# Expert stage of a routed feed-forward layer: 64 tiles of 96 slots against 48 tiles of 128 slots

## What is computed

```python
x = x + tanh(g_xattn) * attention(layernorm(x), ctx)      # channels 128, softmax over 256 keys
t = layernorm(x)                                          # T = 2048 tokens of 256
scores = softmax(t @ gate.T)                              # E = 64 experts, best 3 of 8 groups, top K = 6
pos  = running count of tokens at each expert
slot = expert * C + min(pos, C - 1)                       # C = 96 slots each
buf[slot] = t[token]                                      # the last slot keeps its newest token
out[e] = (silu(buf[e] @ Wg[e].T) * (buf[e] @ Wu[e].T)) @ Wd[e].T     # 256 -> 176 -> 256
y = sum over 6 of out[slot] * weight
x = x + tanh(g_ffn) * (y + shared(t))
```

## Time and profile before

| what | value |
|---|---|
| time, median of 3 runs | 437.4 us (434.9 to 438.97) |
| the profiled execution's own time | 439.52 us |
| its span, first to last instruction | 437.8 us |
| mean granted TensorE clock | 0.946 |
| busy: PE, DVE, POOL, ACT | 342.1, 215.8, 176.3, 155.8 us |
| moved by DMA | 70.50 MB, mean 161 GB/s |

### The profile page before, as it was taken

The page is one execution under the profiler, slowest core; times in us unless marked ns, Lnnn a source line. Parts: engine busy times, 40 slices in busy tenths (PEclk is TensorE's granted clock), DMA queues, the critical chain, the costliest instruction groups (busy, mean ns, idle before and its releaser), DMA issues.

```text
span 437.8 us, 8616 instructions
## 1 busy us (share of the span) xinstructions
PE 342.1 (78%) x2589; PEld 286.3 (65%) x2589; DVE 215.8 (49%) x879; ACT 155.8 (36%) x464; POOL 176.3 (40%) x173
## 2 busy tenths in 40 slices
PE   2779598998999796998987888777968897878600
PEld 1667486876887674886866676666856775767400
DVE  5656568789588888344764111211111211157390
ACT  2566355675466311111423223322323423223000
POOL 3000011010100111022577777776777777776231
PEclk9999979999899999899999899998999999989855
DMA  8798948447100111012598999898899444444797
GB/s 296 285 337 226 266 111 263 125 131 224 58 25 6 49 31 32 25 41 81 142 261 221 250 259 259 215 231 240 216 253 255 76 77 72 73 71 57 178 298 125
DMA packets 36265, 70.50 MB, mean 161 GB/s; under 512 B 6221, under 2 KB 23401, under 8 KB 36231
## 3 DMA queue, kind: packets, MB, share of 16 engines
q1 hardware_dynamic: 21851, 50.56, 37.0%
q0 software_dynamic: 12352, 16.26, 21.2%
q10 hardware_dynamic: 2028, 3.25, 2.3%
HBM read 52.26 MB, written 17.78 MB: 160 GB/s over the span
## 4 chain that ended last, share of the span: by engine, by line
PE 22%; issue 16%; DMA 8%; DVE 7%; POOL 7%; another core or an unknown queue 3%; ACT 2%; SPq 1%; DVEq 0%; ACTq 0%; POOLq 0%
PE bank L347 20%; DMA ctx_sb<-xn_rows,gidx 3%; PE bank L582 2%; DMA w_ring<-third_rows 2%; POOL result L1548 2%; POOL even_rows L1548 2%; DMA qk_sb<-xn_rows,gidx 2%; SPq L321 1%; DMA v_sb<-xn_rows,gidx 1%; POOL third_rows L1548 1%; POOL ctx_sb L1540 1%; DVE hi_hot L1188 1%; DMA even_rows<-x_all,sidx 1%; ACT pt_sb L898 1%
## 5 line engine op out<-in xcount | busy, mean ns | idle before, releaser
L347 PE MATMUL bank<-p_sb,w_ring 128*88 128x96 f32 x1024 | 97.6, 249 | 0.6 <-issue 0.6
L347 PEld LDWEIGHTS bank<-p_sb,w_ring 128*88 128x88 f32 x1024 | 92.0, 160 | 0.9 <-issue 0.8
L1407 DVE TENSOR_TENSOR pt_sb<-pt_sb,bank 88x192 f32<-88x192 f32 x64 | 22.4, 350 | 135.1 <-ACT pt_sb L898 76.4
L1529 POOL TENSOR_SCALAR zeros<-zeros,token 128x256 f16<-128x256 f16 x16 | 14.7, 928 | 155.4 <-DVE zeros L1197 155.4
L347 PE MATMUL bank<-d_ring,pt_sb 88*96 88x256 f32 x256 | 68.7, 392 | 9.5 <-DVE pt_sb L1407 9.5
L898 ACT ACTIVATE pt_sb<-bank 88x192 f32<-88x192 f32 x64 | 20.9, 327 | 94.2 <-PE bank L347 49.7
L347 PEld LDWEIGHTS bank<-d_ring,pt_sb 88*96 88x96 f32 x256 | 37.7, 167 | 19.2 <-DVE pt_sb L1407 11.7
L1548 POOL DMA_INDIRECT even_rows<-x_all,sidx x22 | 31.7, 1439 | 13.3 <-issue 4.9
L893 ACT ACTIVATE p_sb<-bank 128x192 f32<-128x192 f32 x64 | 21.1, 329 | 42.6 <-PE bank L582 22.9
L1548 POOL DMA_INDIRECT third_rows<-x_all,sidx x21 | 30.1, 1435 | 11.1 <-issue 4.0
L1548 POOL DMA_INDIRECT result<-x_all,sidx x21 | 30.2, 1436 | 10.5 <-issue 4.3
(11 more groups left out here) (164 smaller groups left out, 593.6 us busy)
## 6 DMA issues: line engine op xcount, KB each, us to landing
w_ring<-wgu_in SPq DMA_DIRECT2D x32, 704.0 KB
d_ring<-wd_in SPq DMA_DIRECT2D x32, 352.0 KB
even_rows<-zeros SPq DMA_DIRECT2D x1, 2048.0 KB, 7.3
third_rows<-zeros SPq DMA_DIRECT2D x1, 2048.0 KB, 13.4
xn_rows<-xn SPq DMA_DIRECT2D x8, 256.0 KB, 5.0
result<-x_all SPq DMA_DIRECT2D x8, 256.0 KB, 2.2
w_ring<-even_rows SPq DMA_DIRECT2D x4, 512.0 KB, 7.0
w_ring<-third_rows SPq DMA_DIRECT2D x4, 512.0 KB, 7.9
```

Of the source, the lines that this page charges most:

```text
L347: return pe.matmul(o, lhsT, rhs, start=start, stop=stop, skip_group_check=True)
L1407: dve.tensor_tensor(act_tt[:, b % 2, :], silu_sb[:, b % 2, :], eg_ps[b % 2][:, 2 * C:4 * C], ALU.mult)\
L1529: last = pool.tensor_scalar(lo_hot[:, i, :], lo_hot[:, i, :], token1[:, at:at + 1], None, ALU.mult)
```

## The change

The 64 x 96 slots are one row of 6,144 and are cut into 48 tiles of 128; four experts fill three tiles exactly. `gidx` and `sidx` are 128 partitions by 48 tiles. Gathers and adds go by tiles, 7 tiles ahead into 9 buffers, with 4 output buffers. The scatter target is one DRAM tensor `acc_rows` with four regions of 2,176 rows; expert e adds to region e mod 4, so a tile touches two regions, and tiles that touch a common region and could hold a common token wait for each other. All four regions (8.9 MB) are filled with zeros. `down` has its weights stationary and yields the result turned; DVE copies it (`take_ot`), and PE turns it back by tile (`turn_out`). `y` stays in `x_all`: nothing is stored to `result` before the end, where the four regions are read back (2 MB each), DVE adds three to `x_all` and a matmul with the identity adds the fourth to the overflow part in PSUM, and SP stores the result plainly. Tokens lie in DRAM so that a partition's 16 rows are adjacent.

```diff
-SAVED = 4
-AHEAD = 6
-ROWS = 8
-OUTS = 8
+TILES = E * C // P
+TARGETS = 4
+TR = T + P
+AHEAD = 7
+ROWS = ROW_BLKS * EB_TILES
+OUTS = 4
+FILL = TARGETS * TR * L // P // 16
...
-            for d in (even_dram, third_dram):
-                sp.dma_start(d[0:T, :].rearrange("(p a) f -> p (a f)", p=P)
-                             .rearrange("p (a f) -> p a f", a=8), zero8).then_inc(s["fills_in"], 16)
+            for k in range(TARGETS):
+                sp.dma_start(acc_dram.rearrange("(p a) f -> p (a f)", p=P)[:, k * TARGETS * FILL:(k + 1) * TARGETS * FILL]
+                             .rearrange("p (a f) -> p a f", a=TARGETS), zero4).then_inc(s["fills_in"], 16)
...
-                    last = mm(o_ps[b % 2], act_tt[:, b % 2, m * C:(m + 1) * C],
-                              d_ring[:, bass.ds(at + m * L, L)], start=m == 0, stop=m == 1)
+                for h in range(H2):
+                    for m in range(2):
+                        last = mm(ot_ps[e % 2][:, h * C:(h + 1) * C],
+                                  d_ring[:, at + m * L + h * P:at + m * L + (h + 1) * P],
+                                  act_tt[:, e % 2, m * C:(m + 1) * C], start=m == 0, stop=m == 1)
...
+            def turn_out(t):
+                pe.wait_ge(s["ot_out"], last_expert(t) + 1)
+                wait(pe, s["o_ready"], t - 1)
+                for h in range(H2):
+                    last = pe.transpose(o_ps[t % 2][:, h * P:(h + 1) * P],
+                                        turned[t // EB_TILES % 2][:, h, P * (t % EB_TILES):P * (t % EB_TILES + 1)],
+                                        ident[:, :])
...
-            def add_up(e):
-                wait(pool, s["o_ready"], e + 1)
-
-                wait(pool, s[f"acc_in{e % 3}"], 16 * landed(e, e % 3))
+            def add_up(t):
+                pool.wait_ge(s["o_ready"], t + 1)
+
+                i = t % EB_TILES
+                if i < EB_TILES - 1 and t > 1:
+                    pool.wait_ge(s[f"acc_in{(t - 2) % OUTS}"], 16 * ((t - 2) // OUTS + 1))
+                if i == 0 and t > 2:
+                    pool.wait_ge(s[f"acc_in{(t - 3) % OUTS}"], 16 * ((t - 3) // OUTS + 1))
...
+            for r in range(PAIRS):
+                pe.wait_ge(s[f"back2_{r * QUARTERS // PAIRS}"], 16)
+                mm(sum_ps[r][:, :], ident[:, :], back[2][:, 2 * r:2 * r + 2, :].rearrange("p n f -> p (n f)"),
+                   start=False).then_inc(s["ov_done"], 1)
...
-                pool.dma_start(out[P * n * q:P * n * (q + 1), :].rearrange("(n p) f -> p n f", p=P),
-                               even_sb[:, n * q:n * (q + 1), :], accum_op=ALU.add).then_inc(s["result_added"], 16)
+                sp.dma_start(out_to[:, n * q:n * (q + 1), :], x_all[:, n * q:n * (q + 1), :]).then_inc(s["result_out"], 16)
```

More of the change, by code:

```diff
@@ L235, in build @@
[L235 to L242, removed]
+            rows_in0 rows_in1 rows_in2 rows_in3 rows_in4 rows_in5 rows_in6 rows_in7 rows_in8
@@ new lines, in wait_added, with read_back @@
+        def wait_added(eng, t):
+            for k in range(OUTS):
+                wait(eng, s[f"acc_in{k}"], 16 * len(range(k, t + 1, OUTS)))
+        def read_back(eng, k, t):
+            wait_added(eng, t)
+            n = N // QUARTERS
+            for q in range(QUARTERS):
+                eng.dma_start(back[k][:, n * q:n * (q + 1), :],
+                              acc_dram[k * TR:k * TR + T, :].rearrange("(p n) f -> p n f", n=N)[:, n * q:n * (q + 1), :])\
+                    .then_inc(s[f"back{k}_{q}"], 16)
@@ L695, in _ @@
-            for t in range(N):
-                pe.wait_ge(s["w_parts_ready"], t + 1)
-                if t // 2 == 6:
-                    pe.wait_ge(s["o_ready"], E)
-                for k, part in enumerate((high_mid, high_mid, high_low)):
-                    if k == 0 and t in early:
-                        continue
-                    last = mm(bank[t // 2][:, t % 2 * L:(t % 2 + 1) * L], part[:, t * P:(t + 1) * P],
-                              last_parts[:, k, :], start=k == 0, stop=k == 2)
-                last.then_inc(s["ov_done"], 1)
+            turn_rows(1)
@@ new lines, in _ @@
+            for e in range(1, E):
+                if e < E - 1 and last_tile(e + 1) > last_tile(e):
+                    turn_rows(last_tile(e + 1))
+                up(e)
+                down(e - 1)
+                t = last_tile(e - 2) if e > 1 else 0
+                if last_expert(t) == e - 2:
+                    turn_out(t)
+                elif t > 0 and last_expert(t - 1) == e - 2:
+                    turn_out(t - 1)
+            down(E - 1)
+            turn_out(TILES - 2)
+            turn_out(TILES - 1)
@@ new lines, in _ @@
+            take_rows(0)
+            act.wait_ge(s["ht_done"], N)
+            silu(0)
+            take_rows(1)
+            act.wait_ge(s["qk_done"], N)
+            act.wait_ge(s["h_done"], N)
+            for e in range(1, E):
+                if e < E - 1 and last_tile(e + 1) > last_tile(e):
+                    take_rows(last_tile(e + 1))
+                silu(e)
+                t = last_tile(e - 2) if e > 1 else 0
+                if last_expert(t) == e - 2:
+                    take_out(t)
+                elif t > 0 and last_expert(t - 1) == e - 2:
+                    take_out(t - 1)
```

524 lines of the change are left out of this document (282 added, 242 removed).

## The result

| what | before | changed |
|---|---|---|
| time, median (range), same chip | 438.19 us (434.9 to 439.05), 4 runs | 423.38 us (419.24 to 425.65), 4 runs |
| ratio | | 0.9672, 95% interval 0.961 to 0.9734 |
| profiled execution, span | 439.52, 437.8 us | 425.65, 423.9 us |
| second `up` of the stage to the last add | 198.2 us | 177.6 us |
| last add to the end | 31.6 us | 33.7 us |

A forecast was written before the change was run, and what follows sets the result against it. POOL's descriptor making was taken to bound the expert stage. From 439.5 us, stage - 31, opening + 12, middle + 1 and ending + 0.5 gave 422, stated as 421 because that execution ran above the median; range 407 to 443.

The forecast's parts named there:

- POOL bounds the kernel before; fewer, larger indirect transfers free it: Expert stage: POOL's descriptor making sets 2.98 us a pair; 128-row pairs would take 3.3, or 2.48 per expert.
- rival B: Expert stage: descriptors cost in proportion to rows, 3.76 us a pair, so no change at 439 us; chance 0.17.
- PE at 2.55 us is the new floor: Expert stage: PE's `up`, `down` and transposes sum to 2.55 us an expert, 160.7 us for 63.
- 160.7 + 5.5: Expert stage: PE's 63 x 2.55 us, plus 3.5 for last `down`, two turns and copy, and 2 for starts.
- The landing wait costs 1 us: Expert stage under weight loads: adds waiting for earlier adds to land cost 0.03 us over 38 experts, 1 us.
- (L + one pair) / 4: Expert stage: time per expert when adds wait, L being start to landed; (7 + 3.3) / 4 = 2.58 us.
- Rival C: Expert stage: landing wait with L = 10 gives 3.33 us an expert under loads, slower at 449 us; chance 0.15.
- The opening costs 12 us: Opening: larger zero fills ahead of weights and pair 0's store delay every later step by 12 us (9 to 14).
- Rival D: Stage and opening: a pair stays at 2.98 us and the fills are hidden, giving 408 us; chance 0.22.
- The ending gives nothing: Ending: reading back 8.39 MB, last sums and a plain store take 31 to 34 us, no gain; + 0.5 us.
- the middle: Between opening and stage: eight more name matmuls and about three more table operations, 1 us more.

The follow-up runs named there:

- third group: Runs of the unchanged kernel before (444.79 us) and the unchanged changed kernel (424.35 us, ratio 0.9617), each traced again beside a before of 441.56 us.

## Why the prediction came out right, and where it was off

The total, 421 for a measured 423.4, and the direction hold, but its terms were not all of the right size, and that the total came so near is in part luck.

- **POOL bounds the kernel before; fewer, larger indirect transfers free it.** Right in the main: POOL's own work is 180.3 of the 192.9 us between first and last add. The prediction gave it all of them; 12.6 are waits for results. A pair of 128 rows takes 3.17 us, forecast 3.3 from ends of 2.98 and 3.76. That descriptors cost in proportion to rows (rival B) is refuted: 96 to 128 rows adds 0.06 us to a gather, 0.14 to an add.
- **PE at 2.55 us is the new floor.** Right: 2.54, with `down` at 0.89 as forecast. It fits eight weight loads of 128 columns at the 0.111 us of the earlier trace rows. The Trainium skill, "TensorE: Matmul & The Clock Gate", section "LDWEIGHTS (loading the stationary operand)", gives a load by its columns, an estimate of 107 ns for 128; 0.89 / 8 is 111. Streaming alone would have been 0.66. PE's records without a wait or a slow clock make a stage of 164.2 us, 2.0 under the 160.7 + 5.5 of the forecast.
- **The landing wait costs 1 us.** This step failed: it cost 13.4 us in the first trace and 8.0 and 11.1 in the two others of the changed kernel (stages of 177.6, 172.2 and 175.3 against the 164.2 of the runs without wait or load). The form (L + one pair) / 4 was right, but two parts of it were too low. L was put at 7; on the chain the adds' landings are 8.58, 7.97, 8.28, 7.88 and 9.03, mean 8.35. And the 0.76 us from a landing to the next add's start were put at nothing. (8.35 + 0.76 + 3.17) / 4 = 3.07 us an expert, 0.53 over PE's 2.54; POOL's timeline has 3.10, seven blocks of four experts from 224.01 to 310.76. PE felt it as 9.0 us of waiting and 4.3 us by which its records ran longer, most of these at the granted clock of 0.50 behind the two long waits (5.3 and 2.7, and 7.6 and 3.5, in the other traces); the clock was in no term. L breaks even with PE at 4 x 2.54 - 3.17 - 0.76 = 6.2, so the 7 that was chosen already costs 0.2 us an expert, and every microsecond more another 0.25. The prediction had PE feel the wait only when the output buffers run out. In these traces PE waited through gathers queued behind a waiting add; the buffers ran out as well, for ACT, and when the gathers were moved ahead that was the way the wait took. Rival C was this mechanism; its 3.33 us an expert (L = 10) did not come, but 3.10 is nearer to it than to the 2.58 of the forecast.
- **The opening costs 12 us.** Right in kind, too dear: + 4.7 in the first pair of traces, + 9.7 in the second, and the stage began 5 to 9 us before the 221 that the working implies. I took the added bytes in the old shape; the new fills have larger pieces and fewer short tails, and which of the two saved how much is not shown. The run with old-shaped fills measured 11.9, so the term fits those. Rival D (fills hidden by themselves) is refuted, but hiding them by hand works: - 8.1.
- **The ending gives nothing.** Right, + 2.0 for + 0.5, yet for another reason: not the reads of 24 us and two pairs behind them, but DVE's 32 sums, eight pairs of which (10.7 us) come behind the first piece of the last region.
- **The error in the stage (10 too little) and that in the opening (8 too much, with the middle) cancelled** in the first comparison. In the third group, where the old stage was worse, both terms nearly met my figures: - 29.8 for - 31, + 9.7 for + 12.

What stays open: why POOL in the kernel before waits for results 6 us in one run and 20 in another. PE waits for gathers in all three traces, and the granted clock over the first 120 us of the stage is 0.97, 0.93 and 0.97 (first trace, third group, more fills); whether the clock is cause or consequence was not tested.

## What to carry over

When work is cut into fewer, larger indirect transfers, weigh the dependence between them at its landing time under load, not at its quiet one, add the time from the landing to the next start, and compute the point at which it becomes the pitch: near that point take the loss into the sum, with what the clock loses behind PE's waits. Keep what must be early (gathers, first stores) ahead of what may wait in the same queue: moving zero fills behind the first stores, issuing gathers in threes and spreading loads gave 15 us together, nearly as much as the change itself in the same group (17). Before two terms of a forecast are called confirmed, measure each by itself, and measure the kernel before more than once. Idle time beyond an engine's issue gaps, summed over a stage, tells its own work from its waits.

## What the runs showed of the hardware

- With all 16 DMA engines full (share 1.03, 306 GB/s) an indirect add of 128 rows lands 7.4 to 7.8 us after its start in the median; with weights gone, in 3.8. A gather has 6.4 to 6.8 and 3.0. The add that waits for such a landing starts 0.76 us after it.
- Behind waits of PE of 3.58 and 3.01 us the granted clock stood at 0.50, and an `up` took 2.56 us in place of 1.32.
- Making descriptors on POOL is nearly flat in rows: 0.93 to 0.99 us for 96 to 128 rows of 1,280 bytes, 1.44 to 1.58 for adds of 1,024 bytes.
- The same program on the same chip, within one group, came out at a ratio of 1.0106, and the old kernel's medians over groups span 429.2 to 441.6 us; the changed one's span 3.
